# Graph network, four layers: early layer's start, key rows of the edge loop, and the order of scatters

## The reference, cut to what matters

```python
h = relu(layernorm(x))
x = x + relational_attention(h, src, dst, edge_type)   # layer 0
h = relu(layernorm(x)); x = x + gcn_clusters(h)        # layer 1
h = relu(layernorm(x)); x = x + gin_mlp(h, edge_attr)  # layer 2
h = relu(layernorm(x)); x = x + sage(h)                # layer 3

# layer 0: 8 relations, 4 heads of 64
feat_all = einsum('ni,rhid->rnhd', h, conv_weights)
el = sum(feat_all[edge_type, src] * attn_l[edge_type])
er = sum(feat_all[edge_type, dst] * attn_r[edge_type])
e = leaky_relu(el + er)
alpha = softmax of e over the edges with the same dst
out = segment_sum(alpha * feat_all[edge_type, src], dst) + h_bias
# layers 1, 2 and 3 need segment_sum(h[src], dst)
# layer 2 adds, per edge, relu(edge_attr @ w1 + b1) @ w2
```

## Time and profile before

| what | us |
|---|---|
| runs of the kernel | 3144.74, 3149.1, 3156.03 |
| the profiled execution, its own time | 3144.03 |
| its span, first to last instruction | 3142.2 |
| PE busy (matmuls) | 2824.6 (90%) |
| DVE busy | 1831.0 (58%) |
| ACT busy | 1405.3 (45%) |
| POOL busy | 1043.2 (33%) |

### The profile page before, as it was taken

The page is one execution under the profiler, slowest core; times in us unless marked ns, Lnnn a source line. Parts: engine busy times, 40 slices in busy tenths (PEclk is TensorE's granted clock), DMA queues, the critical chain, the costliest instruction groups (busy, mean ns, idle before and its releaser), DMA issues.

```text
span 3142.2 us, 47689 instructions
## 1 busy us (share of the span) xinstructions
PE 2824.6 (90%) x14970; PEld 1862.6 (59%) x15034; DVE 1831.0 (58%) x5208; ACT 1405.3 (45%) x3883; POOL 1043.2 (33%) x1049
## 2 busy tenths in 40 slices
PE   3499958999999999988679998899999999999998
PEld 2344427899999888874144444555555555545446
DVE  7487866888888777775054333355555555513334
ACT  2077866778777888852032000244444444400000
POOL 4266677777777777777000000000000000000000
PEclk6599978999999999977869999999999999999999
DMA  8977754333333333216814333200000000132232
GB/s 295 343 219 204 223 158 117 96 94 95 93 94 92 93 93 94 68 54 181 253 63 123 101 103 98 75 5 7 3 7 5 5 7 3 49 101 68 84 101 79
DMA packets 245039, 317.67 MB, mean 101 GB/s; under 512 B 117627, under 2 KB 165924, under 8 KB 240740
## 3 DMA queue, kind: packets, MB, share of 16 engines
q1 hardware_dynamic: 191412, 179.07, 20.7%
q0 software_dynamic: 49104, 104.11, 11.1%
q10 hardware_dynamic: 4320, 31.95, 2.6%
HBM read 237.42 MB, written 77.59 MB: 100 GB/s over the span
## 4 chain that ended last, share of the span: by engine, by line
PE 63%; DVE 12%; ACT 7%; issue 5%; DMA 5%; SPq 4%; DVEq 3%; POOL 1%; POOLq 0%
PE PS L1237 17%; PE PS L1080 15%; PE PS L954 7%; PE PS L1046 5%; PE PS L1021 4%; PE PS L1059 4%; SPq L360 3%; PE PS L896 3%; DMA BG<-a_d 3%; ACT BG L727 3%; DVE BG L1805 2%; DVEq L1686 2%; DVE SUMS L1671 2%; ACT SL L810 1%; POOL BG L586 1%
## 5 line engine op out<-in xcount | busy, mean ns | idle before, releaser
L575 POOL DMA_INDIRECT a_d<-VAL,IDXS x499 | 501.1, 1004 | 236.9 <-issue 146.0
L1237 PE MATMUL PS<-BG,SL 128*128 128x512 f32 (+1 forms) x1440 | 538.4, 530 | 12.2 <-ACT SL L810 12.2
L586 POOL DMA_INDIRECT BG<-feat_d,IDXST x500 | 490.4, 981 | 155.7 <-issue 127.0
L727 ACT ACTIVATE BG<-BG,SL 128x64 f32<-128x64 f32 x2000 | 513.6, 337 | 0.0
L1671 DVE TENSOR_TENSOR SUMS<-SUMS,PS 128x640 f32 x500 | 409.0, 818 | 156.6 <-PE PS L1021 138.8
L1237 PEld LDWEIGHTS PS<-BG,SL 128*128 128x128 f32 x1440 | 276.4, 194 | 251.8 <-issue 222.4
L618 POOL MEMSET BG<- 128x7680 f32 x1 | 6.5, 6498 | 1254.5 <-DVE MV L1936 1254.5
L1021 PE MATMUL PS<-OHB,BG 128*128 128x128 f32 x2000 | 332.0, 289 | 0.0
L1059 PE MATMUL PS<-OHB,X 128*128 128x128 f32 x2000 | 312.2, 279 | 1.7 <-DVEq L1649 1.7
L1059 PEld LDWEIGHTS PS<-OHB,X 128*128 128x128 f32 x2000 | 282.6, 192 | 14.0 <-issue 1.7
L1046 PE MATMUL PS<-W1A,X 65*128 65x256 f32 x1000 | 271.2, 394 | 4.1 <-ACT X L701 0.9
(11 more groups left out here) (305 smaller groups left out, 4172.7 us busy)
## 6 DMA issues: line engine op xcount, KB each, us to landing
BG<-a_d SPq DMA_DIRECT2D x141, 256.0 KB, 4.2
AL<-a_d SPq DMA_DIRECT2D x137, 256.0 KB, 2.6
a_d<-BG POOLq DMA_DIRECT2D x30, 1088.0 KB, 43.3
feat_d<-SUMS ACTq DMA_DIRECT2D x30, 1040.0 KB
BG<-rel_d SPq DMA_DIRECT2D x100, 160.0 KB
X<-in_edge_attr_dram SPq DMA_DIRECT2D x124, 128.0 KB
SUMS<-a_d SPq DMA_DIRECT2D x52, 256.0 KB, 2.6
SL<-key_d SPq DMA_DIRECT2D x50, 256.0 KB
```

The costliest lines, as they stand in the source:

```text
L575: pool.indirect_dma_start(a_d.rearrange("n (w o) -> (n w) o", o=1), bass.IndirectOffsetOnAxis(ap=IDXS[:, t:t + 1], axis=0), VAL[:, t:t + 1 ...
L586: pool.indirect_dma_start(RING[:, t // NB % 3, t % NB, :], None, feat_d.rearrange("n (r d) -> (n r) d", r=R), bass.IndirectOffsetOnAxis(ap ...
L727: last = act.activation(m, m, ACT.Copy, scale=EXT[:, b % 2, k, 1 + q:2 + q])
L1237: last = pe.matmul(PS[:, to + q, 0:width], lhs[:, i, c, :], w[:, c, q * width:(q + 1) * width], start=(c == 0), stop=(c == kc - 1))
```

## The change

**Prologue.** POOL no longer adds the bias. DVE adds it in 30 steps of the table stage, one tile of X each. POOL's store of X to `xb_d` moves from before scatter 0 to before scatter 128. The twelve small weight loads move on SP's queue from before the table stage to after it. DVE waits for `hb_in` and `n0_hr` in place of `small_in`; the wait for `small_in` stands now in `home` (DVE), after the first `soft_take` (ACT, with the relu of B1C) and before the first `hidden` (PE).

**Edge loop.** PE's turn of the key column is gone. SP loads the keys of the tile as a row to all 128 partitions (64 KB), one of three buffers KROW, once iteration n - 3 has been counted. DVE waits for that load ahead of SAME. The edge attribute loads stand between these loads on SP's queue, one for each four iterations.

**Scatters.** One scatter follows four gathers, in place of two for five, from t = 85 on. The waits on `agg_ps` ahead of the scatters that are left are gone.

```diff
-            with nc.allow_non_contiguous_dma(reason="small weight columns"):
+            def small_weights():
...
                     key_rows(u, b)
+            with nc.allow_non_contiguous_dma(reason="small weight columns"):
+                small_weights()
             sp.wait_ge(s("x_out"), 16)
-            for v in range(NE):
+            def edge_rows(v):
...
+            def key_row(n):
+                c = counted_at(n)
+                if c is not None:
+                    if n >= 3:
+                        sp.wait_ge(s("added"), 10 + n - 2)
+                    load(KROW[n % 3], key_d[c * P:(c + 1) * P].partition_broadcast(P), KROW_IN[n % 3][0])
+            for v in range(3):
+                edge_rows(v)
+            sp.wait_ge(s("dve_mark"), DVE_MARKS["gat_start"])
+            for n in range(T):
+                key_row(n)
+                if n % 4 == 0 and n // 4 + 3 < NE:
+                    edge_rows(n // 4 + 3)
...
-            pool.wait_ge(s("hb_in"), 16)
-            pool.wait_ge(s("n0_hr"), NT)
-            pool.tensor_tensor(X[:, :, :], X[:, :, :], bc(HB.unsqueeze(1), [P, NT, D]), ALU.add).then_inc(s("x_biased"), 1)
...
-            pool.wait_ge(s("x_biased"), 1)
-            pool.dma_start(xb_d.rearrange("(t p) d -> p t d", p=P), X[:, :, :]).then_inc(s("x_out"), 16)
             pool.wait_ge(s("a_zero"), 16 * NT)
             for t in range(SOON):
                 if t % CT == 0:
                     pool.wait_ge(s("val_ready"), t // CT + 3)
+                if t == CT * (NT + 2):
+                    pool.wait_ge(s("x_biased"), NT)
+                    pool.dma_start(xb_d.rearrange("(t p) d -> p t d", p=P), X[:, :, :]).then_inc(s("x_out"), 16)
                 scatter(t)
...
-                if t >= LEAD and (t - LEAD + 1) * 2 // 5 > (t - LEAD) * 2 // 5:
+                if t >= LEAD and (t - LEAD) % 4 == 3:
                     scatter_late(counted)
                     counted += 1
-            for i, n in enumerate(range(counted, TR)):
-                pool.wait_ge(s("agg_ps"), 20 + min(T - 3 * NB + 2 + i, T))
+            for n in range(counted, TR):
                 scatter_late(n)
...
-            act.wait_ge(s("small_in"), 16 * 12)
-            act.activation(B1C, B1C, ACT.Relu).then_inc(s("b1_relu"), 1)
...
             soft_take(0)
+            act.wait_ge(s("small_in"), 16 * 12)
+            act.activation(B1C, B1C, ACT.Relu).then_inc(s("b1_relu"), 1)
...
-                c = counted_at(n)
-                if c is not None:
-                    turn(KEY_AT[n % 3], bc(KEY[:, c:c + 1], [P, P]), P)
...
+            pe.wait_ge(s("small_in"), 16 * 12)
             for q in range(2):
                 hidden(0, q)
...
-            dve.wait_ge(s("small_in"), 16 * 12)
+            dve.wait_ge(s("hb_in"), 16)
+            dve.wait_ge(s("n0_hr"), NT)
...
                 er_step(u, ((u + 1) % 2, (u + 1) // 2))
+                if u < NT:
+                    tt(X[:, u, :], X[:, u, :], HB, ALU.add).then_inc(s("x_biased"), 1)
...
-                        ts(SAME[:, n % 2, :], KEY_AT[n % 3], KEY[:, c:c + 1], 0.0, ALU.is_equal, ALU.add,
+                        rows_sem, before = KROW_IN[n % 3]
+                        dve.wait_ge(s(rows_sem), 16 * (before + n // 3 + 1))
+                        ts(SAME, KROW[n % 3], KEY[:, c:c + 1], 0.0, ALU.is_equal, ALU.add,
```

More of the change, by code:

```diff
@@ L132, in gnn @@
         ONES = sb("ONES", [P, P])
-        TILES = sb("TILES", [1, 3, 1])
-        NEED = sb("NEED", [1, 3, 3])
-        NEEDI = sb("NEEDI", [1, 3, 3], I32)
+        KROWS = sb("KROWS", [P, P])
+        TILES = AL[0:1, 2004:2007].rearrange("o (g k) -> o g k", k=1)
+        NEED = AL[0:1, 2008:2017].rearrange("o (g k) -> o g k", k=3)
+        NEEDI = AL[0:1, 2020:2029].bitcast(I32).rearrange("o (g k) -> o g k", k=3)
         ACC, HS = SUMS[:, 0:3, :], SUMS[:, 3:5, :]
@@ L173, in gnn @@
         EXB = [v.bitcast(BF16) for v in (SLF[:, 1664:1839], BG[:, 15600:15775])]
-        EXR = XF[:, 7528:7528 + NB * (H + 1)].rearrange("p (k c) -> p k c", k=NB)
+        EXR = XF[:, 7296:7296 + NB * (H + 1)].rearrange("p (k c) -> p k c", k=NB)
         DEN = OHB[:, 0:NT * (H + 1)].rearrange("p (t c) -> p t c", t=NT)
@@ L184, in gnn @@
         HOME_LAG = GT + 3
-        KEY, MULT = XF[:, 2560:2560 + T], XF[:, 3060:3060 + T]
+        KEY, MULT = XF[:, 2392:2392 + T], XF[:, 2892:2892 + T]
         KEYT = HSF[0:LT, 6816:7328]
-        SAME = XF[:, 3560:3688].bitcast(BF16).rearrange("p (i n) -> p i n", i=2)
+        SAME = XF[:, 3392:3456].bitcast(BF16)
+        KROW = [XF[:, 7396 + P * i:7396 + P * (i + 1)] for i in range(2)] + [KROWS[:, :]]
+        KROW_IN = [("rows0_in0", IT // 2), ("rows1_in0", IT // 2), ("rows0_in1", IT)]
         BROW = OHB[0:1, 320:320 + T]
@@ L208, in gnn @@
         OHBF = OHB[:, :].bitcast(BF16).rearrange("p (k n two) -> p k n two", k=10, two=2)
-        EA = [XF[:, 3688 + 256 * i:3944 + 256 * i].rearrange("p (k n) -> p k n", k=4) for i in range(3)]
-        EAT = [XF[0:ED + 1, 4456 + 512 * i:4968 + 512 * i].rearrange("p (k n) -> p k n", k=4) for i in range(2)]
-        HM = [XF[:, 5480 + 1024 * i:6504 + 1024 * i].rearrange("p (k n) -> p k n", k=4) for i in range(2)]
+        EA = [XF[:, 3456 + 256 * i:3712 + 256 * i].rearrange("p (k n) -> p k n", k=4) for i in range(3)]
+        EAT = [XF[0:ED + 1, 4224 + 512 * i:4736 + 512 * i].rearrange("p (k n) -> p k n", k=4) for i in range(2)]
+        HM = [XF[:, 5248 + 1024 * i:6272 + 1024 * i].rearrange("p (k n) -> p k n", k=4) for i in range(2)]
         FIRST = BG[0:LT, 3584:3584 + LB * NPAD // 2].bitcast(BF16).rearrange("p (b n) -> p b n", b=LB)
@@ L282, in gnn @@
         SUM_AT = [PSF[:, 1024 * i + P:1024 * i + 6 * P] for i in range(3)]
-        KEY_AT = [PSF[:, 1024 * i:1024 * i + P] for i in range(3)]
         a_set = [sem(f"a_set{k}") for k in range(4)]
@@ L1735, in home @@
             def home():
+                dve.wait_ge(s("small_in"), 16 * 12)
                 step(ts(TILE0, IOTA[0:LT, 0:NT], -float(P), None, ALU.mult))
```

## The result

The changed kernel takes 3174.5 us (median of 6 runs, 3162.4 to 3180.5) against 3149.1 us: a ratio of 1.0074, interval 1.005 to 1.0098. I had forecast 3125 us. The profiled execution spans 3178.7 us, 36.5 more than before. It is the longest of the changed kernel's six, and the profiled one of before, 3144.0 us, lies under all of its runs, so 36.5 is more than the 25.4 us between the medians. The page says little at first sight: PE is busy 90% as before, and the row of the granted clock shows one 8 inside the loop each time, in the seventh slice before and in the ninth now.

The account below looks back on a forecast made before the run. It took the table stage as PE's and a loop batch as shared: 26.74 us DVE plus 9.24 us through ACT and PE. Terms -33.4 + 1 + 2 - 7 + 13 = -24.4 gave 3119.6, on the median 3124.7, forecast 3125 us; range 3106 to 3150.

Parts of the forecast that it names:

- The loop, -7 us forecast: Edge loop: dropping PE's 300 turns was to save 0.45 us in each of 15 batches, 7 us in all.
- only move PE's waiting: Edge loop: in the 26.74 us of a batch when DVE is full, PE's turns cost no time of their own.
- -7, -22, -36: Edge loop: 7 us expected gain, 22 if batches fell to the period without keys, 36 as ceiling by PE alone.
- Rival D: Edge loop: key rows land late and DVE stands; 3165 us at 5 us delay, 3245 at 6; slower, chance 0.09.
- The scatters, +13 forecast: Behind the loop: more scatters are left, so group 3 of the first pass over a_d starts later, costing 13 us.
- E + 163: Behind the loop: the last scatter starts 163 us after E, the end of the loop's last addition.
- -94.5 and 259: Scatters: POOL's last gather waits until some 94.5 us before the loop's end; the 196 scatters left then take 259 us.
- Rival C: First pass over a_d: the 18 us gap follows the last scatter again, +31 in place of +13, 3143 us; chance 0.12.
- The prologue, -33.4 forecast: Before the loop: two pieces save 39.4 us, and 6 come back through DVE's additions and the crowded start.
- the +1 and +2: Prologue: 1 us lost to small weights ahead of the edge rows, 2 us to the store of X behind scatter 127.
- The two pieces: Prologue: no wait for small_in, some 33.3 us sooner, and POOL's bias off DVE's way, 6.1 us; together -39.4 us.
- rival B: Prologue: its covers fail, DVE's additions and the crowded start cost 19 us more, 3144 us; chance 0.10.

## Why the prediction was wrong, point by point

**The loop, -7 us forecast, +36.3 in the profile.** This is the step that failed, the claim that the turns "only move PE's waiting" and that more waiting costs nothing, and none of the term's bounds (-7, -22, -36) reached above zero. The reading of what bounds a batch was right: the four batches without a fall of the clock take 35.4 to 35.8 us, 0.2 to 0.6 less than before, and I had 0.45. Rival D put the danger at late rows; they cost 1.1 us. What I left out is that the 0.12 us turns kept PE at work, and with it the clock up. I counted that PE would wait more, and asked nothing about what a longer wait does. With both the turn and the rows the falls are gone but for one; without rows and without turns they are there.
The Trainium skill, TensorE: Matmul & The Clock Gate, Part 1, says that the throttled state is the default and that activity releases it. The windows above agree in direction: 1.00 up to the pause, 0.50 behind it, and 0.78 once PE has worked on without a break. The profile of before held rows to price it by, and I read neither. PE stood idle from 120 to 140 us at a clock of 0.50. And in the loop itself, in its first batch, ahead of the fourteen compared above, PE paused 6.47 us and its clock fell; only behind it is the clock 1.00 to the loop's end.

```profile
120.00:140.00 20.00, 0.00 (x0) 0.00 (x0) 0.00 (x0) 0.00 (x0) 0.00 (x0) 0.50 1.04 388
...
494.00:508.00 14.00, 9.64 (x40) 9.06 (x41) 6.37 (x19) 3.26 (x11) 10.64 (x12) 0.51 0.44 117
```

```profile
498.36 0.43 PE L896 MATMUL PS<-IDENT,X 128*80 128x128 f32 x1 [6.47 <-DVE X L1583]
```

Whether the pause alone decides or PE's whole load of a batch, is not told apart: pauses of 2.0 us went without a fall as well as with one, 0.94 us always without, 1.3 to 1.5 us mostly without.

**The scatters, +13 forecast, +26.0 in the profile and 23.5 us in its own run.** The last scatter's time, E + 163, was right within 2 us (its own terms, -94.5 and 259, give E + 164.5). The term failed in the landing: 19.3 us in place of 2 to 3. Rival C was near the size (+31) and had the place, without a cause. Its cause is the tile with 122 fillers, as moving that one scatter shows; that the fillers go to one and the same place, and are written one after another for this reason, is my reading of the code and was not tested. With it moved the remaining cost is 7 us in the start of group 3, where I had 12.

**The prologue, -33.4 forecast, -30.4 with the +1 and +2 for what moves past others, -24.4 in the profile.** The two pieces were sized rightly (-38.2 at the first one-hot tile for -39.4; POOL's bias by itself 6.4 for 6.1), the cover was not: I took 9 us in all for what came back (3 for DVE's additions, 3 for the crowded start, 2 for the store of X, 1 for the weights), 14 did. That it lies in the crowded start and in the store of X is argued from the windows and not shown: when the store was spread, its dip went and the time stayed. It is in rival B's direction, 5 us of its 19. The later weights never showed: they were issued by 406 us, in 8 us instead of 46, and nobody waited.

**The sum.** -24.4 + 36.3 + 26.0 - 1.4 = +36.5 us for the profiled execution. The three parts run one by one give -25.7 + 28.5 + 23.5 = +26.3 us, which is the changed kernel's +25.4 between medians, so no fourth cause is needed. Two of the parts gave a loss; the chance of 0.09 for slower stood on a mechanism that did not occur.

## What to carry to other kernels

Taking work away from TensorE can cost time, here 28.5 us: price what its longer wait does to the granted clock, from any idle stretch of the same trace. When a tail of transfers loses its cover, look at the landing time of the very last one, and not at the median of its kind; a stretch behind it in which nothing moves is the hint. A change of several parts is best run part by part: here one part was worth 26 us, and two others ate it.

## What the runs showed that I had not expected

The granted clock fell to 0.50 for 10 to 14 us behind pauses of PE of 1.3 to 2.4 us, at the same work, and cost 4 to 6 us each time; how often it did varies (4 to 8 of 14 batches without turns or fillers, 0 in the kernel before, 1 each in two other kernels with turns). That this makes the changed kernel's runs spread over 18 us isn't shown: 22 runs of the kernel before, beside the scatters' experiments, spread as far, 3138.7 to 3157.1. The scatter of the tile with 6 real edges took 19.3 us to land, the full tile before it 2.1 us. Twelve small weight loads took 46 us to issue among the stores of zeros and 8 us outside them.
